# Attention scores in four PSUM banks instead of two, one bank for each other ring, exponential in the copy of the transposes

## The chip, the cores and the metric

The kernel runs on one core of a Trainium2 chip. The metric is the device time of one execution in microseconds (us). TensorE (PE) multiplies matrices and writes the products to PSUM, which has eight banks of 512 float32 values in each of 128 partitions. VectorE (DVE) and ScalarE (ACT) read PSUM and SBUF; GpSimd (POOL) works from SBUF and issues indirect transfers; SyncE (SP) issues transfers. PEld in a profile is TensorE's weight load.

## What is computed

A cross attention with 16 heads of width 8 on 32 batches of 56 queries, then a mixture of 8 experts, each added to its input:

```python
x = x + xattn(k=ctx, q=layernorm(x), v=ctx, mask)   # causal: key t is seen by queries >= t
    kp, qp, vp = k @ Wk + bk, q @ Wq + bq, v @ Wv + bv          # 16 heads of 8
    att = einsum('bhqd,bhkd->bhqk', qp, kp) / sqrt(8)
    att = softmax(where(causal & mask, att, -1e9))
    y = einsum('bhqk,bhkd->bhqd', att, vp) @ Wo + bo
x = x + moe(layernorm(x))      # softmax gate over 8 experts, top 2, at most 280 tokens an expert,
                               # relu(x @ w1 + b1) @ w2 + b2, weighted by the gate, summed
```

Only the first 56 of 1500 context rows can be seen through the causal mask; a 57th key stands for rows in which everything is masked.

## The kernel before

**Units of work.** Two batches, each padded to 64 rows, make a pair of 128 rows; there are 16 pairs (n). Two pairs make a group (t, 8 of them). A pair's scores are 16 heads by 57 keys, 912 columns a row. A slab is 32 lanes of the projected queries and keys, that is four heads; there are four slabs, and `head_keys` holds the keys spread so that one product over a slab gives four heads, 4 x 57 = 228 columns.

**Order.** Every engine has its own program, written out by hand, and they meet at semaphores. In the attention part a loop over g = 1 to 10 makes one turn for a group on each engine, software-pipelined over four groups. TensorE's turn in its middle form is: transposes of the normalised input of group g+2 (`norm`); the output product `mix` of the odd pair of group g-2; `scores` of the even pair of group g; transposes of the records of group g-3 (`turn_moe`); `values` of group g; transposes of the probabilities (`transpose_probs`, two halves a pair); `gate`; transposes of the attention output (`turn_y`); the rest of the probabilities; projection of queries and keys (`project`); the product with Wo (`output`); `scores` of the odd pair; `ranks`; `mix` of the even pair of group g-1; two more `transpose_probs`. VectorE's turn is: `divide` of the odd pair (reads the product of `mix`), `softmax` of the even pair, `choose`, `residual`, `shift1`, `statistics2`, `slots`, `softmax` of the odd pair, `records`, `statistics1`, `divide` of the even pair. In the last turns the parts of groups that don't exist fall away, and `keep_warm` puts products without use in their place. After the loop come TensorE's waits for the scatter of the tokens, and the eight experts.

**Banks.** Scores take two banks, and only one pair's scores exist at a time: `scores(n)` waits for the subtraction of pair n-1 (`sub_d`). The transposed probabilities take two banks (`probT_b`). The other results of TensorE go through two rings of two banks. `ring_b` serves the kinds k, q, norm, qk, v, y and moe, which ScalarE empties; `post_b` serves mix, gate, wo, rank and two small ones at the start, which VectorE reads. The order of uses is fixed by the tables `RING` and `POST`; in a turn it is norm, moe, v, y, qk and mix (odd), gate, wo, rank, mix (even). TensorE waits until the use before the last has been read:

```python
def take_post(kind, t):
    wait(pe, post_read, POST[kind, t] - 1)
    return post(kind, t)
```

**Scores of a pair.** Two slabs share a bank. So `scores` works in two halves: slabs 0 and 2 together, then slabs 1 and 3 together. A product with the identity lays the mask as a bias into the columns first (`lay_bias`, 456 + 228 columns, then the last 228).

**Softmax.** VectorE reduces the maximum and subtracts it into `probs`; ScalarE applies the exponential in place (`exponential`); TensorE transposes; ScalarE copies the transposes to SBUF (`evacuate`), 512 columns at a time; `mix` multiplies them with the values, which carry a column of ones, so that the row sums come out beside the outputs and `divide` can divide.

## Time and profile before

| | us |
|---|---|
| median of 3 runs | 211.75 (210.69 to 213.86) |
| span of the profiled execution, first to last instruction | 192.6 |
| median less that span | 19.15 |
| TensorE busy | 159.1 (83%) |
| VectorE busy | 110.9 (58%) |
| ScalarE busy | 87.3 (45%) |
| GpSimd busy | 90.7 (47%) |

The record of the profiled execution holds its span but no device time of its own. So what lies around the span is known only against the median, 211.75 - 192.6 = 19.15 us. Busy shares are means over stages: the attention part ends at about 110 us, the scatter of tokens at about 131 us, the experts run from about 139 to 176 us, and the gathering of results fills the rest.

### The profile page before, as it was taken

Reading aid. Unit: us, or ns where it says so; the run is one execution under the profiler, and the core shown is the slowest. Engines: PE = TensorE matmul, PEld = TensorE weight load, DVE = VectorE, ACT = ScalarE, POOL = GpSimd, SP = SyncE. Lnnn points to the kernel's source line nnn. Section 1 sums busy time; section 2 is a strip of 40 time slices with the busy share of each in tenths; the row PEclk is TensorE's granted clock in tenths of the full one; section 3 lists DMA queues with packets and bytes.
Section 4 is the critical chain, followed back from the end, with each engine's and each line's share of the span. In section 5 each row is a group of like instructions: output and inputs, shape, how many; then the busy total and the mean of one; then the engine's idle time right before and its main releaser. Section 6 shows DMA issues by size and latency. Waiting matters only on the chain.

```text
span 192.6 us, 4628 instructions
## 1 busy us (share of the span) xinstructions
PE 159.1 (83%) x1647; PEld 109.8 (57%) x1651; DVE 110.9 (58%) x395; ACT 87.3 (45%) x196; POOL 90.7 (47%) x152
## 2 busy tenths in 40 slices
PE   6588779999999999999999896965399999998000
PEld 2323537777777777767677543422179988886000
DVE  4666534668889888889886553200026554555064
ACT  3547595979797977884735101000123222330000
POOL 4345290014157765757577787761002644656300
PEclk9855766999999999999999999996859999999655
DMA  5910798995000000000100000003700110111666
GB/s 164 327 75 0 300 388 230 338 311 162 0 3 26 31 29 26 14 27 5 37 0 23 4 20 6 16 8 77 198 0 0 44 39 27 31 34 35 240 189 247
DMA packets 10109, 17.96 MB, mean 93 GB/s; under 512 B 1708, under 2 KB 5568, under 8 KB 9576
## 3 DMA queue, kind: packets, MB, share of 16 engines
q1 hardware_dynamic: 6992, 13.58, 21.4%
q0 software_dynamic: 1632, 2.27, 3.9%
q10 hardware_dynamic: 1464, 1.84, 3.0%
q8 instruction: 13, 0.21, 0.5%
q14 instruction: 8, 0.07, 0.1%
HBM read 11.00 MB, written 7.86 MB: 98 GB/s over the span
## 4 chain that ended last, share of the span: by engine, by line
PE 64%; DMA 8%; POOL 7%; issue 6%; ACT 6%; DVE 5%; ACTq 1%; POOLq 1%; DVEq 1%; SPq 0%
PE score_p L977 10%; PE bank L1005 8%; PE bank L1149 7%; PE bank L992 6%; PE score_p L946 5%; PE score_p L1133 5%; PE bank L1133 5%; POOL slots_d L405 3%; PE bank L905 3%; PE bank L938 3%; DMA chosen<-choice_d 3%; DMA xr<-slots_d 2%; PE bank L1022 2%; PE bank L918 2%; DMA choice_d<-rest_ow,rest_i 2%
## 5 line engine op out<-in xcount | busy, mean ns | idle before, releaser
L405 POOL DMA_INDIRECT slots_d<-rec,slot_i x32 | 32.3, 1008 | 13.9 <-issue 12.4
L911 PE MATMUL score_p<-warm 128*128 128x512 bf16 x91 | 24.9, 419 | 6.0 <-DMA slots_d<-rec,slot_i 3.8
L443 POOL DMA_INDIRECT choice_d<-ow,dst_i x16 | 16.0, 1000 | 29.3 <-DVE ow L871 26.4
L674 DVE TENSOR_REDUCE row_max<-score_p 128x16 f32<-128x912 f32 x16 | 17.7, 1104 | 10.6 <-PE score_p L977 10.6
L977 PE MATMUL score_p<-head_keys,queries 32*32 32x228 f32 (+1 forms) x384 | 22.1, 409 | 0.0
L550 ACT ACTIVATE probsT<-bank 128x512 f32<-128x512 f32 x32 | 18.2, 600 | 5.0 <-PE bank L992 4.9
L992 PE MATMUL bank<-ident,probs 128*128 128x128 f32 x128 | 19.6, 291 | 0.0
L911 PEld LDWEIGHTS score_p<-warm 128*128 128x128 bf16 x95 | 9.5, 106 | 16.9 <-DMA slots_d<-rec,slot_i 4.3
L677 DVE TENSOR_TENSOR probs<-score_p,row_max 128x912 f32<-128x912 f32 x16 | 17.7, 1109 | 1.6
L335 POOL TENSOR_TENSOR rs<-ve,minus_half 128x2 f32<-128x2 f32 x8 | 6.3, 791 | 24.8 <-DVE ve L653 21.2
L1005 PE MATMUL bank<-vals,probsT 128*64 128x18 f32 x512 | 17.8, 212 | 0.0
L1005 PEld LDWEIGHTS bank<-vals,probsT 128*64 128x64 f32 x512 | 16.3, 138 | 2.2 <-issue 1.9
L853 DVE TENSOR_SCALAR hid<-score_p,b_s 128x288 f32<-128x288 f32 x8 | 4.1, 517 | 21.9 <-PE score_p L1133 21.9
L541 ACT ACTIVATE probs<-probs 128x912 f32<-128x912 f32 x16 | 15.8, 985 | 1.5 <-DVE probs L677 1.3
L992 PEld LDWEIGHTS bank<-ident,probs 128*128 128x128 f32 x128 | 16.0, 152 | 0.4
L495 ACT ACTIVATE head_keys<-bank,bk_head,wqk_s 128x224 f32<-128x224 f32 x32 | 14.6, 540 | 0.0
L1149 PE MATMUL bank<-w_s,hid 128*128 128x128 f32 x112 | 14.2, 282 | 0.0
L1149 PEld LDWEIGHTS bank<-w_s,hid 128*128 128x128 f32 x112 | 13.6, 199 | 0.2 <-issue 0.2
L946 PE MATMUL score_p<-bias,cb 128*128 128x228 bf16 (+1 forms) x48 | 13.1, 329 | 0.2
L519 ACT ACTIVATE vals<-bank 64x128 f32<-64x128 f32 x32 | 9.0, 282 | 6.1 <-PE bank L938 5.5
L623 ACT ACTIVATE hid<-score_p,b_s 128x288 f32<-128x288 f32 x8 | 4.0, 501 | 16.3 <-PE score_p L1133 16.3
L618 ACT ACTIVATE xgT<-bank 128x256 f32<-128x256 f32 x8 | 3.1, 384 | 17.4 <-PE bank L1105 17.4
(130 smaller groups left out, 281.7 us busy)
## 6 DMA issues: line engine op xcount, KB each, us to landing
choice_d<-chosen SPq DMA_DIRECT2D x2, 1024.0 KB, 8.1
w_s<-w_in SPq DMA_DIRECT2D x1, 2048.0 KB, 8.9
slots_d<-zeros SPq DMA_DIRECT2D x1, 1242.0 KB, 4.4
xg<-slots_d SPq DMA_DIRECT2D x8, 138.0 KB, 4.1
chosen<-choice_d SPq DMA_DIRECT2D x1, 1024.0 KB, 5.0
xs<-x_in SPq DMA_DIRECT2D x1, 768.0 KB, 7.1
ctxT<-ctx_t_in SPq DMA_DIRECT2D x1, 768.0 KB, 8.4
b_s<-b_in SPq DMA_DIRECT2D x1, 512.0 KB, 9.0
```

The lines of the kernel that those rows point to most:

```text
L405: gp.indirect_dma_start(out=slots_d, out_offset=bass.IndirectOffsetOnAxis(ap=slot_i[t % 2][:, k, p:p + 1], axis=0), in_=rec[t % RECS][:, p ...
L443: gp.indirect_dma_start(out=choice_d, out_offset=bass.IndirectOffsetOnAxis(ap=where, axis=0), in_=rows, in_offset=None, bounds_check=N_DST ...
L550: sc.activation(probsT[n % GP][:, 4 * i:4 * i + 4, :].rearrange("a h q -> a (h q)"), probT_b[i][:], ACT.Copy).then_inc(probT_ev, 1)
L674: ve.reduce_max(row_max[:, p, :], heads, X).then_inc(max_d, 1)
L677: ve.tensor_tensor(probs[p][:, :, 0:KEYS], heads, row_max[:, p, :].unsqueeze(2).broadcast_to([128, H, KEYS]), sub).then_inc(sub_d, 1)
L911: mm(bank[0], warm[:, 0:128], warm[:], start=True, stop=True)
L946: mm(score_heads(i)[:, heads, :], ident_b, bias[:, n, 0:KEYS].unsqueeze(1).broadcast_to([128, heads.stop - heads.start, KEYS]), start=True ...
L977: last = mm(score_heads(i)[rows:rows + width, heads, :], queries[t % 2][lanes, asked], head_keys[t % 2][lanes, :, first:first + KEYS], sta ...
L992: last = tr(probT_b[i][:, 128 * h:128 * (h + 1)], probs[p][:, 2 * hp:2 * hp + 2, :].rearrange("q h k -> q (h k)"), ident[:])
L1005: last = mm(to[PAD * j:PAD * (j + 1), VW * hp:VW * (hp + 1)], probsT[p][:, hp, PAD * j:PAD * (j + 1)], vals[t % 2][:, GP * p + j, hp, :], ...
L1133: mm(bank[f][:, 0:SLOTS], w1_s[:, e, 128 * f:128 * (f + 1)], xgT[:, e, :], start=True, stop=True)\
L1149: last = mm(down(e, t), hid[e % HIDS][:, f, 128 * t:128 * (t + 1)], w2_s[:, e, f, :], start=(f == 0 and t == 0), stop=(f == FC - 1), skip_ ...
```

## The change

The scores get four banks, one for each slab. Four bias products of 228 columns are laid, and then eight products follow, for two batches by four slabs, each on 32 lanes and 64 rows. The other two rings shrink to one bank each: a use of `ring_b` or `post_b` waits until the use just ahead of it has been read. VectorE's two passes over the scores read the same 912 columns, from four banks with 228 in each. The exponential in place on ScalarE is gone; `evacuate` applies it instead of a copy, `transpose_probs` waits for the subtraction, and the padding columns of `probs` are set to -1.0e30 instead of 0, so that their exponential is 0. Everything else stays where it is.

```diff
-        score_p = stack.enter_context(nc.psum_tensor("score_p", [128, 2, 512], f32))
-        score_b, probT_b, ring_b, post_b = bank[0:2], bank[2:4], bank[4:6], bank[6:8]
+        score_p = stack.enter_context(nc.psum_tensor("score_p", [128, SLABS, 512], f32))
+        score_b, probT_b, ring_b, post_b = bank[0:4], bank[4:6], bank[6], bank[7]
+        score_v = score_p[:, :, 0:SH * KEYS].rearrange("q i (h k) -> q i h k", k=KEYS)
...
         def ring(kind, t):
-            return ring_b[RING[kind, t] % 2]
+            return ring_b
         def post(kind, t):
-            return post_b[POST[kind, t] % 2]
+            return post_b
...
-            def exponential(n):
-                act.wait_ge(sub_d, n + 1)
-                heads = probs[n % GP][:, :, 0:KEYS]
-                sc.activation(heads, heads, ACT.Exp).then_inc(exp_d, 1)
...
                 sc.activation(probsT[n % GP][:, 4 * i:4 * i + 4, :].rearrange("a h q -> a (h q)"), probT_b[i][:],
-                              ACT.Copy).then_inc(probT_ev, 1)
+                              ACT.Exp).then_inc(probT_ev, 1)
...
-                ve.memset(probs[p][:, :, KEYS:PAD], 0.0).then_inc(probs_clear, 1)
+                ve.memset(probs[p][:, :, KEYS:PAD], GONE).then_inc(probs_clear, 1)
...
             def take_ring(kind, t):
-                wait(pe, ring_ev, RING[kind, t] - 1)
+                wait(pe, ring_ev, RING[kind, t])
             def take_post(kind, t):
-                wait(pe, post_read, POST[kind, t] - 1)
+                wait(pe, post_read, POST[kind, t])
...
                 wait(pe, sub_d, n)
-                lay_bias(n, 0, slice(0, 2 * SH))
-                lay_bias(n, 1, slice(0, SH))
+                for i in range(SLABS):
+                    mm(score_v[:, i], ident_b, bias[:, n, 0:KEYS].unsqueeze(1).broadcast_to([128, SH, KEYS]),
+                       start=True, stop=False, skip_group_check=True)
                 if n % GP == 0:
                     pe.wait_ge(ring_ev, filled("qk" if t else "q", t))
-                for half, width in ((0, PAD), (1, PAD // 2)):
-                    if half:
-                        lay_bias(n, 1, slice(SH, 2 * SH))
-                    heads = slice(SH * half, SH * (half + 1))
-                    for rows in range(0, 2 * PAD, width):
...
-                        for i in range(2):
-                            lanes = slice(SLAB * (2 * i + half), SLAB * (2 * i + half + 1))
+                for j in range(2):
+                    first = 128 * (n % GP) + PAD * j
+                    for i in range(SLABS):
+                        lanes = slice(SLAB * i, SLAB * (i + 1))
+                        last = mm(score_v[PAD * j:PAD * (j + 1), i], queries[t % 2][lanes, first:first + PAD],
+                                  head_keys[t % 2][lanes, :, first:first + KEYS], start=False, stop=True,
+                                  skip_group_check=True)
...
-                pe.wait_ge(exp_d, u // 2 + 1)
+                pe.wait_ge(sub_d, u // 2 + 1)
```

On TensorE, in the turn g = 4, from `mix` of an odd pair (bank<-vals,probsT) through the scores of an even pair and the transposes of `turn_moe` (bank<-ident,rec) to the first product of `values` (bank<-wvo_s,ctxT), before:

```order
L1005 MATMUL bank<-vals,probsT 64x18 [waits post_read,ring_ev,probT_ev]
L1005 MATMUL bank<-vals,probsT 64x18 x15
L946 MATMUL score_p<-bias,cb 128x8x57 [waits sub_d]
L946 MATMUL score_p<-bias,cb 128x4x57
L977 MATMUL score_p<-head_keys,queries 64x4x57 [waits ring_ev]
L977 MATMUL score_p<-head_keys,queries 64x4x57 x3
L946 MATMUL score_p<-bias,cb 128x4x57
L977 MATMUL score_p<-head_keys,queries 32x4x57 x8
L905 MATMUL bank<-ident,rec 128x128 [waits ring_ev,xn2_d]
L905 MATMUL bank<-ident,rec 128x128
L938 MATMUL bank<-wvo_s,ctxT 128x128 [waits ring_ev,meanT_ev]
```

The same place after:

```order
L983 MATMUL bank<-vals,probsT 64x18 [waits post_read,ring_ev,probT_ev]
L983 MATMUL bank<-vals,probsT 64x18 x15
L947 MATMUL score_p<-bias,cb 128x228 [waits sub_d]
L947 MATMUL score_p<-bias,cb 128x228 x3
L955 MATMUL score_p<-head_keys,queries 64x228 [waits ring_ev]
L955 MATMUL score_p<-head_keys,queries 64x228 x7
L895 MATMUL bank<-ident,rec 128x128 [waits ring_ev,xn2_d]
L895 MATMUL bank<-ident,rec 128x128
L928 MATMUL bank<-wvo_s,ctxT 128x128 [waits ring_ev,meanT_ev]
```

The bias is laid in one run of four and the products of all slabs follow in one run of eight, where there were five runs; the waits on `ring_ev` and `post_read` have the same names, but each now asks for a count that is one higher.

On ScalarE, from `empty_moe` (xn2T) to the second copy of transposes in the turn g = 3, before:

```order
L534 ACTIVATE xn2T<-bank 128x256 [waits ring_d]
L519 ACTIVATE vals<-bank 64x2x8x8 [waits post_d,ring_d]
L519 ACTIVATE vals<-bank 64x2x8x8 x3
L528 ACTIVATE yT<-bank,wqk_s 128x256 [waits post_d,ring_d]
L550 ACTIVATE probsT<-bank 128x512 [waits post_d,probT_d]
L541 ACTIVATE probs<-probs 128x16x57 [waits sub_d]
L556 ACTIVATE ratio<-gap 128x2 [waits gap_d]
L550 ACTIVATE probsT<-bank 128x512 [waits post_d,probT_d]
```

The same place after:

```order
L535 ACTIVATE xn2T<-bank 128x256 [waits ring_d]
L520 ACTIVATE vals<-bank 64x2x8x8 [waits post_d,ring_d]
L520 ACTIVATE vals<-bank 64x2x8x8 x3
L529 ACTIVATE yT<-bank,wqk_s 128x256 [waits post_d,ring_d]
L544 ACTIVATE probsT<-bank 128x512 [waits post_d,probT_d]
L550 ACTIVATE ratio<-gap 128x2 [waits gap_d]
L544 ACTIVATE probsT<-bank 128x512 [waits post_d,probT_d]
```

The row of the exponential between the two copies is gone, and the other rows stand as before.

## Rows read from the trace of the kernel before

**Rows 1.** Windows: busy us of each engine in a stretch, then granted clock, DMA.

```profile
55.69:66.33 10.64, 10.64 (x163) 8.01 (x164) 9.49 (x36) 9.13 (x22) 7.57 (x15) 1.00 0.09 26
22.20:25.40 3.20, 1.49 (x9) 0.95 (x7) 1.09 (x5) 3.15 (x8) 2.01 (x3) 1.00 1.05 431
25.60:32.30 6.70, 6.23 (x42) 3.82 (x42) 2.74 (x7) 4.27 (x13) 3.30 (x5) 0.50 0.97 304
32.40:131.30 98.90, 91.86 (x1229) 63.05 (x1230) 67.46 (x260) 57.23 (x129) 57.67 (x107) 1.00 0.18 56
114.30:117.50 3.20, 1.53 (x8) 0.49 (x6) 0.60 (x2) 0.00 (x0) 2.54 (x9) 1.00 0.03 9
```

**Rows 2.** Chain of waits: start, us, what; the odd pair's output product.

```profile
37.24 1.04 PE bank L1005 x32
...
57.98 1.04 PE bank L1005 x32
...
68.62 1.04 PE bank L1005 x32
...
106.52 1.11 PE bank L1005 x32
```

**Rows 3.** Timeline, PE, one turn: start, us, engine, line, operation.

```profile
57.91 1.11 PE L1005 MATMUL bank<-vals,probsT 128*64 128x18 f32 x32
58.95 0.47 PE L946 MATMUL score_p<-bias,cb 128*128 128x456 bf16 x2
59.35 0.61 PE L977 MATMUL score_p<-head_keys,queries 32*64 32x228 f32 x8
...
60.65 0.44 PE L905 MATMUL bank<-ident,rec 128*128 128x128 f32 x2
60.92 0.61 PE L938 MATMUL bank<-wvo_s,ctxT 128*128 128x128 f32 x4
...
62.17 0.42 PE L905 MATMUL bank<-ident,y 128*128 128x128 f32 x2
...
62.88 0.67 PE L918 MATMUL bank<-xnT,wqk_s 128*128 128x256 f32 x2
...
63.77 0.61 PE L1022 MATMUL bank<-wvo_s,yT 128*128 128x128 f32 x4
```

**Rows 4.** Timeline, ACT, the same turn.

```profile
61.12 0.38 ACT L534 ACTIVATE xn2T<-bank 128x256 f32<-128x256 f32 x1 [1.06 <-PE bank L905]
61.57 1.17 ACT L519 ACTIVATE vals<-bank 64x128 f32<-64x128 f32 x4
62.76 0.47 ACT L528 ACTIVATE yT<-bank,wqk_s 128x256 f32<-128x256 f32 x1
...
63.61 0.98 ACT L541 ACTIVATE probs<-probs 128x912 f32<-128x912 f32 x1
```

**Rows 5.** Timeline, DVE, that turn and the beginning of the next.

```profile
59.22 0.48 DVE L641 BATCH_NORM_STATS2 stat<-xs 128x6 f32<-128x128 f32 x2
...
60.20 0.25 DVE L684 RECIPROCAL rden<-bank 128x16 f32<-128x16 f32 x1
...
64.89 0.41 DVE L695 TENSOR_TENSOR x<-x,bank 128x256 f32<-128x256 f32 x1
...
67.21 1.10 DVE L674 TENSOR_REDUCE row_max<-score_p 128x16 f32<-128x912 f32 x1
...
69.96 0.24 DVE L684 RECIPROCAL rden<-bank 128x16 f32<-128x16 f32 x1
...
70.44 0.25 DVE L684 RECIPROCAL rden<-bank 128x16 f32<-128x16 f32 x1
```

**Rows 6.** Timeline, PE, a pair's scores near the start, and what follows.

```profile
16.93 0.76 PE L946 MATMUL score_p<-bias,cb 128*128 128x456 bf16 x2
...
19.84 1.22 PE L938 MATMUL bank<-wvo_s,ctxT 128*128 128x128 f32 x4
```

**Rows 7.** Timeline, DVE, the last group's records.

```profile
116.84 0.60 DVE L709 TENSOR_SCALAR rec<-x,mv,rs 128x128 f32<-128x128 f32 x2 [2.68 <-POOL rs L370]
```

More of the change, by code:

```diff
@@ L207, in build @@
         ring_d, ring_ev, post_d, post_read = (sem(n) for n in ("ring_d", "ring_ev", "post_d", "post_read"))
-        score_d, max_d, sub_d, exp_d = (sem(n) for n in ("score_d", "max_d", "sub_d", "exp_d"))
+        score_d, max_d, sub_d = (sem(n) for n in ("score_d", "max_d", "sub_d"))
         probT_d, probT_ev, rden_d, y_d = (sem(n) for n in ("probT_d", "probT_ev", "rden_d", "y_d"))
@@ L569, in _ @@
             empty_qk(1)
-            exponential(0)
             empty_v(0)
@@ L575, in _ @@
             empty_norm(2)
-            exponential(1)
             normalise(3)
@@ L587, in _ @@
                 evacuate(4 * (g - 1) + 2)
-                exponential(GP * g)
                 if 0 <= g - 3 < GROUPS:
@@ L597, in _ @@
                 evacuate(4 * g + 1)
-                exponential(GP * g + 1)
                 if 0 <= g + 3 < GROUPS:
@@ L940, in values @@
                 last.then_inc(ring_d, 1)
-            def score_heads(i):
-                return score_b[i].rearrange("q (h k) -> q h k", k=PAD)[:, :, 0:KEYS]
-            def lay_bias(n, i, heads):
-                mm(score_heads(i)[:, heads, :], ident_b,
-                   bias[:, n, 0:KEYS].unsqueeze(1).broadcast_to([128, heads.stop - heads.start, KEYS]),
-                   start=True, stop=False, skip_group_check=True)
             def scores(n):
```

19 lines of the change are left out of this document (6 added, 13 removed).

## Prediction

> **What bounds the kernel now.** I read the windows of the stretch in the middle of the attention part first. One turn there lasts 10.64 us, and TensorE is busy for all of it; VectorE is busy for 9.49 and ScalarE for 9.13 [rows 1]. The chain of waits says the same from another side: the odd pair's output product stands in it at 57.98 and again at 68.62, one turn apart, and all that it names in between is TensorE [rows 2]. The timeline shows why VectorE's slack of about 1 us is thin: its divisions of the even pair (69.96) and of the odd pair (70.44) stand back to back, right behind the softmax of the odd pair that began at 67.21 [rows 5]. So TensorE bounds the attention part and VectorE is a close second. The granted clock is at 2.4 GHz from 32.4 us to the scatter, and was at 1.2 GHz before [rows 1]. The change touches nothing in the experts, so what it does shows up to about 131 us.
>
> **What it saves.** A pair's scores on TensorE last from 58.95 to 60.65, 1.70 us [rows 3]. The first bias run ends and the first products start at 59.35, 0.40 later; those eight records end 0.61 later, and both halves last about the same, though one has eight records and the other sixteen. The time of such a run is therefore that of one stream and its fill, not of the number of tiles. The new run has sixteen records on all four slabs. If the slabs run side by side it takes the 0.55 us from start to start of one half; if they go two by two it takes 1.1. I take 0.55, since two slabs that write two banks already run together. Bias: 912 columns as before, 0.50 with the switch behind it. New scores: 1.05, a saving of 0.65 a pair and 1.3 a turn. On this point the Trainium skill, TensorEngine Tiling (Array Packing), section Restrictions and Gotchas, says that row tiles may run at once only into different banks, which is the packing that the change makes; the two slabs of a half agree with it, and no row shows four at once.
>
> The exponential takes 0.98 us of ScalarE a pair [rows 4]. It goes; the copy of the transposes, which takes the exponential over, I leave at its time, with 0.1 us either way for the other function. ScalarE waited 1.06 us for work in this turn [rows 4], so the saving shortens no path, but it takes about 1 us off the way from softmax to transposes, which TensorE did not wait for. VectorE's two passes still read 912 columns each; from four banks instead of two I take them at the same time, and bound it at plus or minus 0.1 us each. Padding with another constant costs nothing.
>
> **What it adds: one bank each for two rings.** Before, TensorE filled one bank while the other was emptied. Now each use waits for the read of the one just before. The places where this bites are read in the order of the turn:
>
> - v behind moe. The transposes of the records start at 60.65 and the values at 60.92, directly behind [rows 3]. Now the values wait until ScalarE has emptied xn2T (0.38 us) [rows 4].
> - y behind v. ScalarE needs 1.17 us to empty the values [rows 4]; TensorE has only the transposes and the gate between.
> - qk behind y: yT takes 0.47 us [rows 4].
> - mix of the odd pair behind the division of the even pair. Before, this product started at 57.91, while the same turn's even division ran at 60.20, 2.3 us later [rows 3, 5]. Now it waits for it. Queued behind the waiting product on TensorE are the scores of the next even pair, and VectorE waits with empty hands, since what stands next in its order is the division of that very product.
> - residual reads the product with Wo, which lies behind all three ring waits on TensorE; statistics, slots, the odd softmax and the even division are queued behind residual on VectorE.
>
> So the two engines, which ran side by side, now take turns on one loop. I walk it from one start of the odd product to the next. A handoff from one engine to another and back I take at 0.18 us for the pair (0.03 shows from the record transposes' end, 61.09, to xn2T at 61.12; the way back with a weight load that is no longer done ahead I estimate at 0.15).
>
> TensorE: mix 57.91 to 58.95, 1.04; new scores 1.05; record transposes 0.44; xn2T 0.38 and handoffs 0.18; values 0.61; their copies 1.17 and 0.18; y transposes 0.42; yT 0.47 and 0.18; projections 62.88 to 63.77, 0.89; product with Wo 0.61. Together 7.62. VectorE: handoff 0.04; residual to odd row maximum, 64.89 to 67.21, 2.32; odd softmax and records, 67.21 to 69.96, 2.75; even division to its read, 0.56; handoff back 0.15. Together 5.82. **The loop is 13.44 us, against 10.64: plus 2.8 a turn** [rows 3, 4, 5]. The 1.3 us saved is in this sum by half only: the odd pair's scores run beside VectorE's statistics.
>
> Over the kernel: the odd product stands at 37.24 in turn 2 and at 106.52 in turn 9, 69.3 us for seven turns [rows 2]. Turn 2 has no records, choice or slots, but has input statistics, 59.22 to 60.20, 0.98 [rows 5]: about 12.7. Turn 3 has everything and these statistics: 14.4. Turns 4 and 5: 13.4 each. Turns 6 and 7 have no projection: 12.55 each. Turn 8 has no scores, softmax or values: about 8.3. Sum 87.3, plus 18.0. In the start the ring waits add about 1 (the transposes of the first input must wait for the four copies of the keys), and the shorter scores give most of it back at 1.2 GHz: plus 0 to 2, I take 1. At the end something comes back: the last group's records wait 2.68 us for GpSimd's power, which stands behind the scatters of the group before [rows 7]; with longer turns GpSimd has no backlog. Minus 2. **Without a change of the clock: +17, 211.75 + 17 = 229 us.** By the span that is 192.6 to about 210.
>
> **The clock.** TensorE now pauses at several places in each turn. Before the values it is 0.56 us. Before y it is 1.35 less the work that lies between, 61.53 to 62.17, so 0.7; before the projections 0.65 less 62.59 to 62.88, so 0.36. From the end of Wo's product, 64.38, to the odd product at 68.62 TensorE had 4.24 us of work and has 3.6 with the shorter scores; VectorE needs 5.82, so 2.2 us of pause lie there, split before the even and the odd product, and 3.2 with input statistics [rows 2, 3, 5]. From 22.2 to 25.4 it was busy for 1.49 of 3.20 us at the high clock, and from 25.6 to 32.3 it ran at the low one; from 114.3 to 117.5 it was busy for 1.53 of 3.20 and kept the high one [rows 1]. So pauses of this size can cost the clock and need not. The turn 2 to 3 and the turn 3 to 4 are the ones with the longest pause, since the input statistics lengthen VectorE's part. The price: at the low clock a pair's scores took 16.93 to 19.84, 2.91 against 1.70 [rows 6, 3], and TensorE's terms in the loop, 1.04, 1.05, 0.44, 0.61, 0.42, 0.89, 0.61, are 5.06 and nearly double. One turn at the low clock costs 4 to 5 us, and a low clock makes TensorE busier, which brings the high one back. I expect one or two such turns: +7, **236 us**. The Trainium skill, TensorE: Matmul & The Clock Gate, section A second HAM failure mode: psum-queue depth-cycling, describes this very thing, small idle times between groups of products that cycle through PSUM banks and a clock that falls and rises with them; the figure there is not used.
>
> **Rivals.**
>
> 1. Loop as above, clock falls once or twice: 236. Chance 0.50.
> 2. Loop as above, clock stays: 229. For it speaks the stretch at 114.3. Chance 0.33.
> 3. The slabs don't run side by side: 0.53 more a turn on the loop and some on the other pair, 4 to 5 in all on top of either, 234 to 242. Against it speaks that two slabs do. Chance 0.08.
> 4. Not slower: the read of the even pair is early enough to hide the new wait. It would have to be done at 57.91, where the odd product stands now, and it is done at 60.20 + 0.56, 2.9 us late. Were VectorE's order such that this wait is gone, and the ring's waits were covered by other products, VectorE would be the bound at about 9.8 a turn (9.49 busy and the small gaps between dependent operations, an estimate), and the kernel would win 0.8 in each of seven turns: 206. It decides on where the division stands in VectorE's order, which the change leaves. Chance 0.03 for faster, 0.04 for anything in between, within 2% (a measurement of this kernel can tell about 2%, 4 us).
> 5. Something else on the slow side, such as a clock that stays low through most turns: 250 or more. Chance 0.02.
>
> **Range.** From 225 (rival 2 with a bigger give-back, handoffs of half the size over some 30 of them) to 246 (rival 1 with slabs in twos, or three turns at the low clock). Faster 0.03, same 0.04, slower 0.93.
>
> **What the profile after would show.** The odd output product's starts 13 to 14.5 us apart in the middle turns. The wait of the odd product for the even division, 1 us or more a turn, as the largest idle time of TensorE; values waiting for xn2T, y for the copies of the values. VectorE's residual waiting for the product with Wo. Sixteen records of scores from start to end in 0.6 us at the high clock. ScalarE idle for several us a turn. A granted clock of 0.5 in part of 37 to 80 us for rival 1. The last records with little wait for GpSimd. The experts unchanged. I am wrong if the turns are 11 us or less, in which case VectorE's divisions are done earlier than I read, or if they are over 16 with the high clock, in which case a wait is there that I have not seen.

## The result and the profile after

The changed kernel takes 234.4 us, median of 4 runs (232.62 to 235.16), beside 211.47 us (210.69 to 213.86) for the kernel before: a ratio of 1.1219, 95% interval 1.1128 to 1.131. It is slower, by 22.9 us. The profiled execution took 235.16 us with a span of 233.4, so 1.8 us lie around the span. Of some kernels below a few executions take over 1.5% more than the fastest (in e6 three of four, in e11 two of four); ratios and intervals leave them out, medians and differences in us don't.

The page of the changed kernel: busy time by engine, the granted clock in 40 slices, and the groups that answer to the changed lines.

```profile
PE 176.2 (75%) x1539; PEld 128.0 (55%) x1539; DVE 111.9 (48%) x395; ACT 73.7 (32%) x180; POOL 91.0 (39%) x152
...
PEclk9956587695696799996556957559997699999955
...
L983 PE MATMUL bank<-vals,probsT 128*64 128x18 f32 x512 | 21.5, 230 | 15.0 <-DVE y L678 8.3
...
L664 DVE TENSOR_REDUCE row_max<-score_p 128x16 f32<-128x912 f32 x16 | 17.6, 1102 | 10.9 <-PE score_p L955 10.9
L544 ACT ACTIVATE probsT<-bank 128x512 f32<-128x512 f32 x32 | 18.0, 597 | 11.6 <-PE bank L970 11.3
...
L667 DVE TENSOR_TENSOR probs<-score_p,row_max 128x912 f32<-128x912 f32 x16 | 17.7, 1109 | 1.6
...
L535 ACT ACTIVATE xn2T<-bank 128x256 f32<-128x256 f32 x8 | 3.1, 384 | 45.2 <-PE bank L895 40.7
L674 DVE RECIPROCAL rden<-bank 128x16 f32<-128x16 f32 x16 | 4.1, 255 | 25.5 <-remote 14.6
```

The same three groups on the page of the kernel before:

```profile
L674 DVE TENSOR_REDUCE row_max<-score_p 128x16 f32<-128x912 f32 x16 | 17.7, 1104 | 10.6 <-PE score_p L977 10.6
...
L550 ACT ACTIVATE probsT<-bank 128x512 f32<-128x512 f32 x32 | 18.2, 600 | 5.0 <-PE bank L992 4.9
...
L677 DVE TENSOR_TENSOR probs<-score_p,row_max 128x912 f32<-128x912 f32 x16 | 17.7, 1109 | 1.6
```

The two passes over the scores take 1102 and 1109 ns, where they took 1104 and 1109, and the copy of the transposes with the exponential in it takes 597 ns, where it took 600: VectorE reads four banks as fast as two, and the other function costs nothing. The output product (L983) has 15.0 us of idle time ahead of it, 8.3 of them for `y` of a division. It is the largest idle time on TensorE, as forecast. ScalarE waits 45.2 us ahead of xn2T. The clock row (PEclk, tenths of full speed in 40 slices) has many fives and sixes where the attention part lies.

One turn on TensorE, the timeline from odd product to odd product.

```profile
85.72 1.11 PE L983 MATMUL bank<-vals,probsT 128*64 128x18 f32 x32 [1.33 <-DVE y L678]
...
87.27 0.64 PE L955 MATMUL score_p<-head_keys,queries 32*64 32x228 f32 x16
87.84 0.44 PE L895 MATMUL bank<-ident,rec 128*128 128x128 f32 x2
90.17 0.68 PE L928 MATMUL bank<-wvo_s,ctxT 128*128 128x128 f32 x4 [1.89 <-ACT xn2T L535]
...
92.19 0.41 PE L895 MATMUL bank<-ident,y 128*128 128x128 f32 x2 [0.56 <-ACT vals L520]
...
93.25 0.67 PE L908 MATMUL bank<-xnT,wqk_s 128*128 128x256 f32 x2 [0.22 <-ACT yT L529]
...
94.14 0.61 PE L1000 MATMUL bank<-wvo_s,yT 128*128 128x128 f32 x4
...
96.94 1.11 PE L983 MATMUL bank<-vals,probsT 128*64 128x18 f32 x32 [0.86 <-DVE slot_e L733]
...
100.61 1.11 PE L983 MATMUL bank<-vals,probsT 128*64 128x18 f32 x32 [1.53 <-DVE y L678]
```

This answers to the turn in [rows 3]. The sixteen records of scores now take 0.57 us from their start to the next row's start (87.27 to 87.84), on all four slabs at once. The waits of the forecast are all there: values for xn2T, the transposes of y for the copies of the values, the projections for yT, the even product for the slots that stand ahead of it on VectorE, and the odd product for the even division (1.53 us). One turn takes 14.89 us, against 10.64 in [rows 1].

The same turn on VectorE, ScalarE and GpSimd, where one wait is not explained by the program.

```profile
89.40 0.26 DVE L674 RECIPROCAL rden<-bank 128x16 f32<-128x16 f32 x1 [3.83 <-remote]
...
94.86 0.42 DVE L685 TENSOR_TENSOR x<-x,bank 128x256 f32<-128x256 f32 x1 [1.15 <-PE bank L1000]
```

```profile
89.64 0.38 ACT L535 ACTIVATE xn2T<-bank 128x256 f32<-128x256 f32 x1 [4.50 <-PE bank L895]
```

```profile
87.69 0.97 POOL L406 DMA_INDIRECT slots_d<-rec,slot_i  x1 [0.30 <-issue]
```

The odd product's last record ends at 86.83, but the division that reads it starts at 89.40, and the profile puts the release down to nothing on this core ("remote"). xn2T starts at 89.64 though its transposes ended at 88.28. Both start 0.7 to 1.0 us after the last scatter (`DMA_INDIRECT` on GpSimd) of the turn ends (87.69 + 0.97 = 88.66). The same pattern stands in four turns of this trace, where the division starts 1.8 to 2.6 us after the product's end; with what it waits anyway that is the 14.6 us of idle time by the page.

The windows of that turn and of one stretch at the low clock.

```profile
85.72:100.61 14.89, 9.83 (x144) 7.85 (x145) 8.88 (x31) 6.33 (x16) 6.79 (x14) 1.00 0.05 16
106.40:126.80 20.40, 18.74 (x156) 14.87 (x155) 11.33 (x44) 6.31 (x17) 7.69 (x15) 0.50 0.04 10
```

The second window shows 1.2 GHz for 20.4 us on end, and five more such stretches of 6.8 to 13.7 us lie between 38 and 158 us. That is not the one or two turns of the forecast.

### The profile page after: what moved, and what is told of

The parts are those of the page before. It is cut to its first block, busy times and chain, and to the rows that moved or that the text cites. A ratio compares the mean times of both kernels' runs of the same rounds, so it can differ in the third digit from the quotient of the medians.

```text
span 233.4 us, 4392 instructions
## 1 busy us (share of the span) xinstructions
PE 176.2 (75%) x1539; PEld 128.0 (55%) x1539; DVE 111.9 (48%) x395; ACT 73.7 (32%) x180; POOL 91.0 (39%) x152
## 4 chain that ended last, share of the span: by engine, by line
PE 54%; DVE 12%; issue 10%; DMA 8%; ACT 6%; POOL 4%; another core or an unknown queue 2%; POOLq 1%; ACTq 1%; DVEq 1%; SPq 0%
PE score_p L1111 8%; PE bank L983 6%; PE bank L1127 6%; PE bank L895 5%; PE bank L970 5%; PE score_p L955 4%; PE bank L928 4%; PE score_p L901 4%; PE score_p L947 3%; DVE row_max L664 3%; DMA xr<-slots_d 2%; PE bank L1000 2%; PE bank L908 2%; DMA chosen<-choice_d 2%; POOL slots_d L406 2%
## 5 line engine op out<-in xcount | busy, mean ns | idle before, releaser
L406 POOL DMA_INDIRECT slots_d<-rec,slot_i x32 | 32.2, 1007 | 14.6 <-issue 12.5
L983 PE MATMUL bank<-vals,probsT 128*64 128x18 f32 x512 | 21.5, 230 | 15.0 <-DVE y L678 8.3
L901 PE MATMUL score_p<-warm 128*128 128x512 bf16 x95 | 29.5, 465 | 3.2 <-DMA slots_d<-rec,slot_i 1.7
L983 PEld LDWEIGHTS bank<-vals,probsT 128*64 128x64 f32 x512 | 20.2, 163 | 17.7 <-issue 11.4
L970 PE MATMUL bank<-ident,probs 128*128 128x128 f32 x128 | 25.3, 349 | 0.0
L664 DVE TENSOR_REDUCE row_max<-score_p 128x16 f32<-128x912 f32 x16 | 17.6, 1102 | 10.9 <-PE score_p L955 10.9
L970 PEld LDWEIGHTS bank<-ident,probs 128*128 128x128 f32 x128 | 21.0, 187 | 0.7 <-issue 0.5
L843 DVE TENSOR_SCALAR hid<-score_p,b_s 128x288 f32<-128x288 f32 x16 | 8.2, 516 | 23.9 <-PE score_p L1111 23.7
L1111 PE MATMUL score_p<-xgT,w_s 128*128 128x288 f32 x64 | 18.9, 443 | 0.5 <-issue 0.5
L901 PEld LDWEIGHTS score_p<-warm 128*128 128x128 bf16 x95 | 10.3, 115 | 16.0 <-issue 6.2
L667 DVE TENSOR_TENSOR probs<-score_p,row_max 128x912 f32<-128x912 f32 x16 | 17.7, 1109 | 1.6
L535 ACT ACTIVATE xn2T<-bank 128x256 f32<-128x256 f32 x8 | 3.1, 384 | 45.2 <-PE bank L895 40.7
L674 DVE RECIPROCAL rden<-bank 128x16 f32<-128x16 f32 x16 | 4.1, 255 | 25.5 <-remote 14.6
L1111 PEld LDWEIGHTS score_p<-xgT,w_s 128*128 128x128 f32 x64 | 12.6, 208 | 3.9 <-issue 0.9
L613 ACT ACTIVATE hid<-score_p,b_s 128x288 f32<-128x288 f32 x16 | 8.0, 501 | 20.9 <-PE score_p L1111 20.9
```

What stands on the lines that cost most here:

```text
L406: gp.indirect_dma_start(out=slots_d, out_offset=bass.IndirectOffsetOnAxis(ap=slot_i[t % 2][:, k, p:p + 1], axis=0), in_=rec[t % RECS][:, p ...
L664: ve.reduce_max(largest, score_v, X).then_inc(max_d, 1)
L667: ve.tensor_tensor(probs[p][:].rearrange("q (i h) k -> q i h k", h=SH)[:, :, :, 0:KEYS], score_v, largest.unsqueeze(3).broadcast_to([128, ...
L901: mm(bank[0], warm[:, 0:128], warm[:], start=True, stop=True)
L970: last = tr(probT_b[i][:, 128 * h:128 * (h + 1)], probs[p][:, 2 * hp:2 * hp + 2, :].rearrange("q h k -> q (h k)"), ident[:])
L983: last = mm(to[PAD * j:PAD * (j + 1), VW * hp:VW * (hp + 1)], probsT[p][:, hp, PAD * j:PAD * (j + 1)], vals[t % 2][:, GP * p + j, hp, :], ...
```

## Experiments

A setting is one chip at one time: e1 to e4 ran on one chip, e5 to e8 and e9 to e12 on another at two times, and the result above is from the first setting. Each setting ran the kernel before as well. The kernel before took 191.04 us beside e1 to e4, 193.01 beside e5 to e8 and 191.51 beside e9 to e12 (medians of 7), so all differences below are to the one of the same setting.

**e1_same** is the kernel before, unchanged.

> The kernel before, unchanged, to see the span and the granted clock of each of its executions. Its profiled execution had a span of 192.6 us at a mean granted clock of 0.885, while the median of the times is 211.5 us; the four executions of the changed kernel all have a span just 1.8 us under their time. Theory A: the timed executions of the kernel before run with spans near 209 us at a mean clock under 0.85, so that the clock already falls in the kernel before in most executions, and its profiled execution was an unusual one. Theory B: they have spans near 193 us like the profiled one, and 17 to 19 us lie outside the span; then the changed kernel's loss would be 40 us of span and less outside it.

Measured: 191.83 us (189.58 to 193.51), ratio 1.0002 (0.9885 to 1.0118), span 189.1. The time is 1.8 us above the span, and the span is near the 192.6 of the profile shown. So the profile of 192.6 us was no unusual one, and the kernel before has no 19 us outside its span here. What it did in the first setting, theory A or theory B, this run can't tell.

**e2_ring** gives the one ring one bank, and nothing else.

```diff
-            return ring_b[RING[kind, t] % 2]
+            return ring_b[0]
-                wait(pe, ring_ev, RING[kind, t] - 1)
+                wait(pe, ring_ev, RING[kind, t])
```

> The kernel before with one bank for ring_b alone, everything else as before. If the loop of the prediction holds, the three waits for ScalarE stretch TensorE's turn by 0.56 + 0.7 + 0.36 = 1.6 us in about seven turns and something at the start: plus 10 to 12 us at the same clock. If the loss of the changed kernel comes from post_b alone, plus 3 us or less. If the clock already varies from run to run, somewhat less than 10.

Measured: 209.66 us (208.73 to 210.57), ratio 1.1023 (1.0936 to 1.1109), +18.6 us. One turn on TensorE:

```profile
66.32 1.11 PE L1005 MATMUL bank<-vals,probsT 128*64 128x18 f32 x32
...
70.07 0.68 PE L938 MATMUL bank<-wvo_s,ctxT 128*128 128x128 f32 x4 [0.56 <-ACT xn2T L534]
...
72.09 0.41 PE L905 MATMUL bank<-ident,y 128*128 128x128 f32 x2 [0.56 <-ACT vals L519]
...
73.15 0.67 PE L918 MATMUL bank<-xnT,wqk_s 128*128 128x256 f32 x2 [0.22 <-ACT yT L528]
...
79.08 1.11 PE L1005 MATMUL bank<-vals,probsT 128*64 128x18 f32 x32
```

The turn is 12.76 us at the high clock, 2.1 more than before. The three ring waits are there with 0.56, 0.56 and 0.22 us, where the prediction had 0.56, 0.7 and 0.36, and in other turns up to 0.44 us more for the copies of the keys. From the odd product to the projections it is 6.83 us (66.32 to 73.15) against 4.97 in [rows 3], so 1.86 of the 2.1 us lie at these three places: each costs more than the idle time shown. The odd product stands at 41.78 in turn 2, against 37.24 in [rows 2]: with the old scores, the start costs 4.5 us, not 1 (and 6.3 against e1, where it stands at 35.50). Besides the start, two stretches of 3.4 us each (from 85.0 and from 98.6) were at the low clock. The cost, forecast at 10 to 12 us, was underrated.

**e3_post** gives the other ring one bank, and nothing else.

```diff
-            return post_b[POST[kind, t] % 2]
+            return post_b[0]
-                wait(pe, post_read, POST[kind, t] - 1)
+                wait(pe, post_read, POST[kind, t])
```

> The kernel before with one bank for post_b alone. The loop theory: TensorE and VectorE take turns (even division, odd product, odd division), plus 2 to 2.5 us a turn, plus 14 to 18 us in all. If the ring's waits are the larger part, plus 7 or less. The sum of this run and the one on the ring should be more than the changed kernel's 23 us, since they share their slack and the changed kernel has shorter scores.

Measured: 226.19 us (225.78 to 230.48), ratio 1.1885 (1.1787 to 1.1983), +35.2 us. The output products on TensorE:

```profile
71.37 1.11 PE L1005 MATMUL bank<-vals,probsT 128*64 128x18 f32 x32 [2.31 <-DVE y L688]
...
81.81 1.11 PE L1005 MATMUL bank<-vals,probsT 128*64 128x18 f32 x32 [0.56 <-DVE slot_e L743]
...
85.50 0.70 PE L1005 MATMUL bank<-vals,probsT 128*64 128x18 f32 x18 [1.32 <-DVE y L688]
```

The waits for the division (y) are those of the changed kernel, and the one for the slots is a little shorter; the turn shown is 14.13 us, with the low clock from 73.5 to 76.9. Five more stretches between 39 and 135 us were at 1.2 GHz. The cost is twice what was expected, and this edit alone costs at least as much as the whole change does in e5 (ratios 1.1885 and 1.1744, with intervals that overlap).

**e4_exp** moves the exponential into the copy, and nothing else.

```diff
-                sc.activation(heads, heads, ACT.Exp).then_inc(exp_d, 1)
...
-                              ACT.Copy).then_inc(probT_ev, 1)
+                              ACT.Exp).then_inc(probT_ev, 1)
```

> The kernel before with the exponential in the copy of the transposes alone (and the padding at -1.0e30), two banks for the scores and for each ring as before. Prediction's view: ScalarE has slack, so nothing, within plus or minus 2 us. Rival: it shortens the way from softmax to the transposes and takes waits away from TensorE at the start, where nothing is overlapped: 2 to 4 us faster. If the exponential out of PSUM costs more a column than a copy: ScalarE's rows over 0.7 us and no gain.

Measured: 190.71 us (189.49 to 192.92), ratio 1.0005 (0.9901 to 1.0109). ScalarE around the place where the exponential stood:

```profile
60.24 0.38 ACT L534 ACTIVATE xn2T<-bank 128x256 f32<-128x256 f32 x1 [2.20 <-PE bank L894]
...
63.78 0.20 ACT L549 ACTIVATE ratio<-gap 128x2 f32<-128x2 f32 x1 [0.94 <-DVE gap L715]
```

ScalarE now waits 2.20 us for xn2T's transposes and 0.94 us more later, where [rows 4] have 1.06 us and the exponential's 0.98. The time that it saved became idle time.

**e5_after** is the changed kernel again, beside the kernel before in a new setting.

> The changed kernel itself, beside the kernel before in the same rounds. The four runs before this one had the unchanged kernel at 191 us, where the result had it at 211.5. If what differs is the whole setting, 234 * 191 / 211.5 = 212 us. If it is the kernel before that varies from setting to setting while the changed one does not, 230 to 236 us again; its span in the result, 233.4 us, lies 40.8 us over the span of 192.6 in the profile of the kernel before, so I expect the latter.

Measured: 224.98 us (224.47 to 225.96), ratio 1.1744 (1.1661 to 1.1827), +32.0 us by the medians and some 33 by the ratio. Neither of the two values expected came out: the changed kernel got faster in the new setting too, by less than the kernel before. The turn at the high clock, TensorE and then VectorE:

```profile
86.24 1.11 PE L983 MATMUL bank<-vals,probsT 128*64 128x18 f32 x32 [1.32 <-DVE y L678]
...
87.79 0.64 PE L955 MATMUL score_p<-head_keys,queries 32*64 32x228 f32 x16
88.36 0.44 PE L895 MATMUL bank<-ident,rec 128*128 128x128 f32 x2
89.36 0.68 PE L928 MATMUL bank<-wvo_s,ctxT 128*128 128x128 f32 x4 [0.56 <-ACT xn2T L535]
...
91.39 0.41 PE L895 MATMUL bank<-ident,y 128*128 128x128 f32 x2 [0.56 <-ACT vals L520]
...
92.45 0.67 PE L908 MATMUL bank<-xnT,wqk_s 128*128 128x256 f32 x2 [0.22 <-ACT yT L529]
...
96.13 1.11 PE L983 MATMUL bank<-vals,probsT 128*64 128x18 f32 x32 [0.85 <-DVE slot_e L733]
...
99.80 1.44 PE L983 MATMUL bank<-vals,probsT 128*64 128x18 f32 x24 [1.53 <-DVE y L678]
```

```profile
87.39 0.26 DVE L674 RECIPROCAL rden<-bank 128x16 f32<-128x16 f32 x1 [1.30 <-PE bank L983]
...
94.06 0.42 DVE L685 TENSOR_TENSOR x<-x,bank 128x256 f32<-128x256 f32 x1 [1.61 <-PE bank L1000]
...
99.08 0.25 DVE L674 RECIPROCAL rden<-bank 128x16 f32<-128x16 f32 x1
```

There is no unexplained wait: the division starts at 87.39, right behind the product, and the turn takes 13.56 us. It is TensorE until residual starts (86.24 to 94.06, 7.82) and VectorE until the next odd product (94.06 to 99.80, 5.74). The windows of this turn and of three low stretches:

```profile
52.10:62.30 10.20, 9.63 (x70) 7.68 (x67) 4.02 (x15) 3.05 (x9) 1.33 (x4) 0.50 0.01 2
69.20:79.40 10.20, 9.29 (x75) 7.44 (x76) 4.23 (x16) 3.05 (x9) 3.09 (x6) 0.50 0.07 21
86.24:99.80 13.56, 9.83 (x144) 7.85 (x145) 9.06 (x31) 6.33 (x16) 6.78 (x14) 1.00 0.05 18
99.90:110.10 10.20, 9.63 (x80) 7.81 (x80) 4.28 (x16) 3.05 (x9) 3.08 (x5) 0.50 0.05 15
```

At the high clock TensorE is busy for 9.83 of 13.56 us, and behind that turn the clock is at 1.2 GHz again. All of 11.1–21.4, 24.8–31.6, 38.4–41.9, 52.1–62.3, 69.2–79.4, 99.9–110.1, 116.9–123.8, 130.6–134.0 and 140.8–144.3 us were at the low level; from 38.4 to 144.3 us, that is 48 us. Each of the last seven stretches begins between 0.4 us ahead of the start of an odd product and 1.3 us behind it, so at the end of the turn's longest pauses or just behind it. The odd product at 86.24 us alone has no fall behind it. Between 144.3 us and the end two more of 3.4 us follow, and the kernel before has such stretches there too.

**e6_both** has the edits of e2 and e3 together, with the scores and the exponential as before.

> The kernel before with one bank for each of the two rings, two banks of scores in halves and the exponential in place as before. So what is left of the change is only what takes time away by the prediction. The loop theory: the changed kernel plus 0.65 us a turn for the even pair's longer scores and up to 1 us a turn for the exponential where it now lies on the loop, 5 to 8 us above the changed kernel. In the trace of the changed kernel a second thing shows: the odd pair's output product ends at 86.8 us and the division that waits for it begins at 89.4, and so in three other turns, 1.8 to 2.6 us each; the semaphore updates of that product, of the scores behind it and of the record transposes all come together there. The run with one bank for post_b alone has no such gap. If the gap belongs to the new scores or the new exponential, this run has none, and comes out within 3 us of the changed kernel or below it. If it belongs to one bank for both rings, it shows here too.

Measured: 241.83 us (237.57 to 244.11), 1.253 times the median before, +48.8 us. By the fastest of its executions, 237.57 us, the new scores and the new exponential together give back 12.6 us of what the two rings cost (237.57 - 224.98), where 5 to 8 were expected. Its trace has no late start of the division either (93.50, behind the product of 92.34 to 93.45).

**e7_halves** is the changed kernel with its products in another order.

```diff
-                for j in range(2):
-                    first = 128 * (n % GP) + PAD * j
-                    for i in range(SLABS):
+                for j, i in [(j, i) for part in ((0, 2), (1, 3)) for j in range(2) for i in part]:
+                    first = 128 * (n % GP) + PAD * j
+                    if True:
```

> The changed kernel with the eight products of a pair in another order: slabs 0 and 2 first, then slabs 1 and 3, still in four banks and one run. If four slabs at once are what holds the updates of the products in front of them (the gap of 1.8 to 2.6 us between the odd product's end and the division), the gap goes and the kernel is 6 to 10 us faster. If the order does not matter, within 2 us of the changed kernel, with the same run of 0.6 us for sixteen records.

Measured: 228.46 us (226.42 to 230.66), ratio 1.1884 (1.1756 to 1.2012), 3.5 us above e5, with intervals that overlap. In the traces the sixteen records take the same 0.57 us (89.50 to 90.07), the turn at the high clock 13.57 us (87.95 to 101.52), and the seven turns 103.15 us (39.17 to 142.32) against 103.14 in e5; only the start is 1.7 us longer. So no gain is seen, and the order of the slabs is not what makes the change slow. The gap that this run was to close is absent in e5 already, so that question fell away.

**e8_order** is the changed kernel with the even division ahead of the odd softmax on VectorE.

```diff
+                if 0 <= g - 1 < GROUPS:
+                    divide(GP * (g - 1))
                 softmax(GP * g + 1)
                 if 0 <= g - 2 < GROUPS:
                     records(g - 2)
                 if 0 <= g + 4 < GROUPS:
                     statistics1(g + 4)
-                if 0 <= g - 1 < GROUPS:
-                    divide(GP * (g - 1))
```

> The changed kernel with one thing moved on VectorE: the division of the even pair stands ahead of the softmax of the odd pair instead of behind records and statistics. The loop theory says that TensorE's wait for that division is the dearest part: the odd product can then run beside the softmax. VectorE waits 1.2 us for the even product in exchange. A turn should fall from 14.9 to 12.5 us or less, 15 to 22 us less than the changed kernel in all. If the ring's waits or the clock are the dearest part, less than 5 us.

Measured: 205.58 us (204.19 to 208.78), ratio 1.0701 (1.0608 to 1.0794), 19.4 us below e5. The window of the attention part, and one turn on TensorE:

```profile
33.40:142.60 109.20, 86.83 (x1138) 62.74 (x1136) 68.39 (x260) 43.78 (x113) 57.55 (x107) 1.00 0.16 50
```

```profile
71.32 1.11 PE L983 MATMUL bank<-vals,probsT 128*64 128x18 f32 x32 [0.86 <-DVE slot_e L733]
...
73.61 1.11 PE L983 MATMUL bank<-vals,probsT 128*64 128x18 f32 x32
75.34 0.57 PE L947 MATMUL score_p<-bias,cb 128*128 128x228 bf16 x4 [0.62 <-DVE probs L667]
...
84.19 1.02 PE L983 MATMUL bank<-vals,probsT 128*64 128x18 f32 x29 [0.85 <-DVE slot_e L733]
```

From 33.4 to 142.6 us the clock was at 2.4 GHz. The odd product (73.61) follows the even one (71.32) without a wait, and in place of 0.85 and 1.32 us the turn has pauses of 0.86 (for the slots) and 0.62 (for the softmax), beside the three of the ring, which stay at 0.56, 0.56 and 0.22. From even to even product the turn is 12.87 us, and in e5 13.57 at the same clock (82.56 to 96.13). How much of the 19.4 us is shorter turns and how much the clock, the next experiment parts.

**e9_fill** is the changed kernel with useless products in the pauses of turns 2 to 7: ten of 128x512 a turn, six ahead of the odd product and two at each of two other places.

```diff
+            def fill(g, n, to, sem, value):
+                if not 2 <= g < GROUPS:
+                    return
+                pe.wait_ge(sem, value)
+                for _ in range(n):
+                    mm(to[:, 0:512], warm[:, 0:128], warm[:], start=True, stop=True)
...
+                fill(g, 6, bank[0], sub_d, GP * g)
                 mix(GP * (g - 2) + 1)
...
+                fill(g, 2, probT_b[0], probT_ev, 4 * (g - 1) + 2)
                 if 0 <= g < GROUPS:
                     values(g)
...
+                fill(g, 2, probT_b[0], probT_ev, 4 * (g - 1) + 4)
                 mix(GP * (g - 1))
```

> The changed kernel with products without use in TensorE's pauses of the turns g = 2 to 7: six of 512 columns before the odd output product, two before the values, two before the even output product, each behind a wait that the next real product has anyway or that is over earlier. No wait of the kernel goes away, so by the loop theory the turn at the high clock stays at 13.6 us. If the low clock in five stretches of the attention part costs 12 us or so, this kernel is 8 to 13 us faster than the changed one, and its granted clock stays at 1.0 from about 35 us to the scatter. If the clock costs nothing because the waits hide it, within 2 us, or slower by what the fillers add.

Measured: 214.55 us (213.79 to 217.32), ratio 1.1205 (1.1111 to 1.1299), against 1.1744 in e5: 0.054 of some 192 us, 10.4 us less. Windows of the attention part and of one turn:

```profile
33.40:122.10 88.70, 76.50 (x1015) 54.04 (x1014) 58.32 (x195) 40.45 (x104) 37.38 (x71) 1.00 0.18 57
80.77:94.64 13.87, 12.11 (x156) 8.53 (x155) 9.05 (x31) 6.32 (x16) 6.78 (x14) 1.00 0.05 17
```

TensorE is busy for 12.11 of 13.87 us and the clock stays at 2.4 GHz until 122.1 us. The useless products cost 0.3 us in this turn (13.56 in e5), so the low clock costs at least 10 us of e5's 32, and the waits, less what the shorter scores save, about 22. By the odd products the seven turns take 91.4 us here (39.15 to 130.54), 103.1 in e5 (37.47 to 140.61) and 82.3 in e8 (37.70 to 119.96). So of e8's gain of 20.9 in the turns, some 9 are shorter waits, less what the useless products cost, and some 12 are the clock.

**e10_both_exp** is e6 with the exponential in the copy: the changed kernel but for its scores.

> The kernel before with one bank for each of the two rings and the exponential in the copy, but scores in two banks and halves as before. Against the run with both rings and the old exponential (241.8 beside 193.0) it prices the exponential where the overlap is gone; against the changed kernel (225.0 beside 193.0) it prices the new scores. Loop theory: the exponential lies beside TensorE's waits and is worth 0 to 3 us; the new scores take 0.65 us off each turn, and the clock with them, so that the other 14 to 17 us would have to be theirs. If the exponential matters more than I thought, 8 us or more below the run with both rings.

Measured: 239.91 us (238.52 to 242.98), ratio 1.252 (1.2411 to 1.2629). Against e5's 1.1744 the new scores are worth about 15 us; the exponential is worth nothing that shows. By the odd products' starts, turn 2 begins at 43.04 (37.47 in e5), and the seven turns take 112.0 us (103.1). Of the 12.6 us between the two spans (236.7 and 224.2), 5.6 are won in the start, where much of the time the clock is at the low level, and 8.9 in the turns, and 1.9 are lost behind them. With e6 the new scores are worth 12 to 15 us.

**e11_post_order** is e3 with the moved division of e8.

> The kernel before with one bank for post_b, as in the run that was 35 us slower, but with the division of the even pair ahead of the odd pair's softmax on VectorE. If the price of that bank is the place of the division in VectorE's order, 20 us or more of the 35 go, leaving VectorE's wait of 1.2 us a turn for the even product: 200 to 206 beside 192. If it is the single bank as such, less than 10 us go.

Measured: 206.71 us (204.16 to 209.71), ratio 1.0719 (1.0594 to 1.0843). Of the 35 us that one bank costs this ring, some 22 hang on where the division stands in VectorE's order (0.1885 - 0.0719 = 0.117 of 191 us), as expected. How much of them is the clock is not parted here.

**e12_early** is e8 with the values moved ahead of the odd product on TensorE, and their copies ahead of xn2T on ScalarE.

```diff
+                if 0 <= g < GROUPS:
+                    values(g)
                 mix(GP * (g - 2) + 1)
                 scores(GP * g)
...
-                if 0 <= g < GROUPS:
-                    values(g)
                 transpose_probs(4 * (g - 1) + 2)
```

> The changed kernel with the moved division, and the projection of the values placed ahead of the odd output product on TensorE and ScalarE, so that its four copies run beside that product and the scores and neither the record transposes nor y wait for them. Two of the three ring waits (0.56 and 0.56 us a turn) should go and half a wait for the copy of the normalised input come in. Theory that the ring's waits lie on the loop also after the division is moved: 3 to 6 us faster than the run with the moved division (205.6 beside 193.0). Rival: VectorE is the bound there, and nothing changes, or it gets slower by the new wait. To beat the kernel before, it would have to gain 13 us, which I don't expect.

Measured: 208.98 us (207.87 to 209.91), ratio 1.0925 (1.0838 to 1.1011), 3.4 above e8 by the medians and some 4 by the ratios, in another setting: a miss. Windows of one turn and of one stretch at the low clock:

```profile
49.40:59.60 10.20, 10.20 (x79) 8.38 (x80) 5.02 (x22) 3.04 (x9) 2.08 (x5) 0.50 0.01 2
78.48:89.62 11.14, 9.69 (x145) 7.79 (x144) 7.83 (x31) 6.12 (x16) 5.74 (x13) 1.00 0.05 18
```

The turn at the high clock did get shorter, 11.14 us, where the same turn of e8 takes 12.65 (73.61 to 86.26). But turn 3 of e12, with the low clock from 49.4 to 59.6, takes 15.69 against 12.17, turn 8 takes 11.41 against 9.73, and turn 2 begins 1.5 us later (39.16, 37.70). The clock took back more than the edit gave. Just ahead of 49.4 us e12 has a pause that e8 has not: the values of that turn now wait 0.84 us for the copy of the normalised input (until 49.27), after 0.69 us ahead of the transposes (until 48.02). In e8 only the 0.69 stands there (until 48.23). That this pause brought the clock down is not shown.

No kernel of these beat the one before.

## Why the prediction held, and where it did not

The time, 236 forecast and 234.4 measured, the direction and the range held. The parts, by the prediction's steps:

- **The loop.** Forecast 13.44 us a turn at the high clock, TensorE 7.62 and VectorE 5.82; e5 has 13.56, with 7.82 and 5.74. The walk from one odd product to the next, handoff by handoff, is what made this part of the forecast good. Only its turn 8 was clearly too short: 8.3, where e8 has 9.73 at the high clock.
- **The wait of the odd product** for the even division: named as the largest, and shown twice to be the one. Moving the division gives 19.4 us (e8 against e5) and some 22 us (e11 against e3); in e8 the shorter waits themselves are 9 us of it or less, and the clock, which then stays high, the rest. The pauses ahead of the even and the odd product were forecast at 2.2 us together; e5 has 0.85 + 1.32 to 0.85 + 1.54.
- **The slabs run together** (rival 3 is out): sixteen records in 0.57 us, the 0.55 that was taken. Yet what the new scores are worth as a whole, 12 to 15 us (e6 and e10 against e5), is more than the prediction gave them. Its half of 1.3 us a turn would be 0.65 in each of seven turns, 4.6; between the traces of e10 and e5, 5.6 us come from the start, much of it at the low clock, and 8.9 from the turns, with stretches at the low clock in both kernels.
- **The start.** Forecast plus 0 to 2; the odd product of turn 2 is at 37.47 in e5 against 37.24 in [rows 2] and 35.50 in e1: plus 0.2 to 2.0. The sum was right, its two terms were too small: the ring waits cost 4.5 to 6.3 (e2), and the scores give 5.6 back (e10).
- **The exponential and VectorE's passes**: worth and cost nothing, as said (e4; 1102 and 1109 ns against 1104 and 1109).
- **The end.** Forecast minus 2. The wait of the last records for GpSimd fell from the 2.68 us of [rows 7] to 0.27 in e5. From the odd product of turn 9 to the end of the span it is 83.6 us in e5 (140.61 to 224.2), and was 86.1 (106.52 to 192.6): minus 2.5. In e1 it is 84.3 (104.8 to 189.1), which makes it minus 0.7, so this term is not shown to better than 2 us.
- **The clock** is the term that was mis-sized. "One or two such turns: +7" was forecast. In e5 the seven turns take 14.17, 17.91, 16.69, 13.56, 15.79, 14.48 and 10.54 us, 103.1 in all; the walk gave 12.7, 14.4, 13.4, 13.4, 12.55, 12.55 and 8.3, 87.3. One turn has no low clock and is right within 0.2. The six others hold all of the excess of 15.8, some 1.5 to 3.5 each. With the clock held (e9) the turns are 13.2, 14.6, 13.9, 13.9, 13.0, 12.7 and 10.2, and their sum of 91.4 is 4 above the walk, half of it in turn 8, which had no useless products and 0.83 as its mean clock. So of the excess some 12 us are the clock (103.1 - 91.4), 0.3 to 3.4 in each of the six turns, and the rest is the walk's own, with what the useless products cost. The price of a turn, 4 to 5, was too high and the number of turns far too low. By its mechanism the outcome lies between rival 1 (once or twice) and rival 5 (low through most turns, chance 0.02), at a time that fits rival 1.

The reason given for one or two turns was the stretch in [rows 1] with 1.53 of 3.20 us busy that kept the high clock. A single stretch of that kind said nothing of a turn that has such pauses each time: in e5 the clock came back and fell again in six turns of seven. The Trainium skill, TensorE: Matmul & The Clock Gate, section A second HAM failure mode: psum-queue depth-cycling, names frequent small idle times between groups of products as a cause of a clock that goes up and down; e5 agrees with it, with seven low stretches from 38.4 us on, and so does e9, where filling the pauses ended it in the turns that were filled. e8 doesn't follow: it has small pauses at five places a turn and kept the high clock.

**The base was off as well.** The forecast of +24 was put on 211.75. In the settings in which the kernel before takes 191 to 193 us, which is what its shown span of 192.6 fits, the change costs 32.0 us (17.4%) and the changed kernel takes 225: 8 us more than the forecast +24. In the first setting the kernel before took 18 us more than there and the changed one 9 more. That 236 and 234.4 agree to 1% is therefore in part luck: a clock term of 7 us for 12 and a walk that was 2 to 4 us short in seven turns, and against them a base of 211.75 that e1 didn't bear out. In the profile of the result the seven turns take 106.2 us (37.77 to 144.01), 3.1 more than in e5. Behind them it is 89.4 us against 83.6, with 1.2 GHz from 143.9 to 157.6 us, so most of what the first setting added there is not in the loop at all.

What stays open: why the first setting was slower for both; the releases that came late there (below); and what decides whether the clock falls, with e2, e8 and e12 side by side. Whether the late releases also lengthened the runs of the kernel before in the first setting can't be told, since no span of those runs is known.

## What to carry to other kernels

A PSUM bank taken from a ring can turn each reader of that ring into a wait of TensorE, so before trading one away, look where the reader of the last use stands in its engine's order: here moving one division was worth 19 us of 32, over half of it by the clock. Then walk the new loop once with the durations of the trace, engine by engine, and count the pauses in it: if each turn has some, don't count on the high clock, and price both cases: it fell in six turns of seven in e5, twice in e2 and in none in e8. Useless products in the pauses (e9) tell what the clock costs. And check the base: a median that stands 19 us above the span of the same kernel calls for a new measurement of that kernel before a difference is put on top of it.

## What the runs showed of the hardware

- **A release that came late.** In the first setting's trace of the changed kernel, four turns have VectorE start 1.8 to 2.6 us after the product that it waits for (86.83 to 89.40 in the turn shown), and ScalarE 0.4 to 1.5 us after its own (88.28 to 89.64), each time 0.7 to 1.0 us after the last scatter of the turn ended. The same kernel in another setting (e5) has none of it (the division 0.04 us behind the product), with the same scatters in the same place of the turn (the last one from 88.21). It costs 1.3 us in the turn shown (14.89 against 13.56). Its cause was not found.
- **Four slabs at once.** From their start to the next row's start, sixteen records in four banks take 0.57 us, and eight records in two banks took 0.55 (59.35 to 59.90 in the trace of before); by the rows' own durations it is 0.64 and 0.61. Each record uses 32 rows of the array.
- **The clock with small pauses.** In e5 TensorE was busy for 9.83 of 13.56 us, in pieces, with no pause over 1.6 us, and the granted clock fell behind it; in e9, busy for 12.11 of 13.87, it stayed. But in e8, busy for 10.06 of 12.90 in a turn, it stayed too, through 109 us. And in e2 it fell at 85.0 us, though TensorE had been busy for 9.11 of the 10.3 us before, with no pause over 0.56 us. So neither the busy share nor the longest pause puts these four in order, and no run here separates what does.
